# One core: the sixth expert's low parts move from GpSimd to VectorE, and the sorted tokens are routed earlier

## What is computed

```
x = conv_attention(x)               # 1x1 convolutions, batch norm, softmax over 256 pixels, plus x
t = tokens(x)                       # 4 x 256 = 1024 tokens of 128 numbers
t = t + attention(layer_norm(t))    # causal mask, softmax over the queries
t = t + experts(layer_norm(t))
x = images(t)

def experts(z):                     # 8 experts of 128 -> 512 -> 128; each token uses its best 2
    logits = z @ Wg
    top, index = top_k(logits, 2);  w = softmax(top)
    out = 0
    for e in range(8):
        out += cw[:, e] * (silu(z @ W1[e]) @ W2[e])   # cw: w where e was chosen, otherwise 0
    return out
```

## Time and profile before

| what | value |
|---|---|
| median of 3 runs | 128.77 us |
| the three runs | 128.94, 127.63, 128.77 us |
| the profiled execution's own time | 127.66 us |
| its span, first to last instruction | 125.9 us |
| PE busy | 106.8 us, 85% |
| VectorE busy | 91.7 us, 73% |
| ACT busy | 80.5 us, 64% |
| GpSimd busy | 56.0 us, 44% |
| TensorE clock granted | 1.00 in every stage |

### The profile page before, as it was taken

How to read it: one execution, slowest core, us unless ns; L and a number is a source line. 1 busy time by engine, 2 the same in 40 slices (tenths; PEclk the granted TensorE clock), 3 DMA queues, 4 the chain that set the end, 5 groups by cost and what they waited for, 6 DMA issues and landing times.

```text
span 125.9 us, 3269 instructions
## 1 busy us (share of the span) xinstructions
PE 106.8 (85%) x1077; PEld 86.4 (69%) x1077; DVE 91.7 (73%) x310; ACT 80.5 (64%) x193; POOL 56.0 (44%) x96
## 2 busy tenths in 40 slices
PE   5568589699976999999999299689799999999760
PEld 1366469587865599898887177488678877878530
DVE  0264778898799984999476956978998878876720
ACT  4226998548666767988968278657375757575511
POOL 6835752849988500007778845303303330332000
PEclk9999999999999999999999999999999999999999
DMA  2338999970000000000121158000010000000003
GB/s 84 100 88 244 317 343 332 299 175 3 5 0 0 0 0 5 3 0 22 43 68 44 43 131 239 0 0 0 28 43 3 5 0 0 5 0 5 0 0 104
DMA packets 12549, 8.75 MB, mean 70 GB/s; under 512 B 1139, under 2 KB 11350, under 8 KB 12534
## 3 DMA queue, kind: packets, MB, share of 16 engines
q1 hardware_dynamic: 12070, 7.86, 22.1%
q0 software_dynamic: 416, 0.68, 1.7%
q10 hardware_dynamic: 48, 0.02, 0.1%
HBM read 6.20 MB, written 2.35 MB: 68 GB/s over the span
## 4 chain that ended last, share of the span: by engine, by line
PE 43%; DVE 24%; issue 12%; POOL 11%; ACT 5%; DMA 2%; POOLq 0%; ACTq 0%; DVEq 0%
PE bank L1628 7%; POOL rows_dram L677 6%; PE bank L1614 5%; PE bank L1602 3%; PE bank L1604 3%; PE bank L1603 3%; POOL fg L696 2%; DMA xT<-in_x_dram 2%; PE bank L1618 2%; PE bank L1661 2%; DVE acc L1311 2%; DVE st L993 2%; PE bank L1705 2%; PE bank L1707 2%; PE bank L1706 2%
## 5 line engine op out<-in xcount | busy, mean ns | idle before, releaser
L688 POOL TENSOR_TENSOR hidl<-hid,hidh 128x512 f16<-128x512 f32 x8 | 9.2, 1154 | 26.6 <-ACT hid L837 26.6
L835 ACT ACTIVATE hidh<-bank 128x512 f16<-128x512 f32 x17 | 10.2, 597 | 14.0 <-PE bank L1604 13.9
L677 POOL DMA_INDIRECT rows_dram<-rows,slot_at x10 | 11.4, 1135 | 16.1 <-issue 16.1
L1602 PE MATMUL bank<-zg,W1h 128*128 128x128 f16 x68 | 12.6, 220 | 1.6 <-DVE zg L1238 1.6
L1661 PEld LDWEIGHTS bank<-W2f,hid 128*128 128x128 f32 x96 | 12.8, 192 | 1.0
L1661 PE MATMUL bank<-W2f,hid 128*128 128x128 f32 x96 | 13.3, 275 | 0.0
L881 ACT ACTIVATE hid<-bank 128x384 f32<-128x384 f32 x22 | 10.7, 489 | 3.4 <-PE bank L1707 2.3
L1603 PE MATMUL bank<-zg,W1h 128*128 128x128 f16 x68 | 12.6, 219 | 0.0
L1604 PE MATMUL bank<-zg,W1l 128*128 128x128 f16 x68 | 12.6, 219 | 0.0
L878 ACT ACTIVATE hidh<-bank 128x384 f16<-128x384 f32 x16 | 7.8, 489 | 5.4 <-PE bank L1707 4.1
L1614 PE MATMUL bank<-W2hl,hidh 128*128 (+1 forms) x68 | 10.6, 275 | 0.8 <-DVE outl L1263 0.8
(11 more groups left out here) (261 smaller groups left out, 356.0 us busy)
## 6 DMA issues: line engine op xcount, KB each, us to landing
W1f<-in_L_ffn_W_dram SPq DMA_DIRECT2D x8, 256.0 KB, 5.4
W2f<-in_L_ffn_W_dram SPq DMA_DIRECT2D x8, 256.0 KB, 6.0
rows_dram<-zero_row SPq DMA_DIRECT2D x1, 1122.0 KB, 10.1
xg<-rows_dram SPq DMA_DIRECT2D x3, 264.0 KB, 3.7
xT<-in_x_dram SPq DMA_DIRECT2D x2, 256.0 KB, 2.9
out_dram<-total SPq DMA_DIRECT2D x3, 128.0 KB, 1.8
xg<-rows_dram SPq DMA_DIRECT2D x1, 198.0 KB, 2.9
rows_dram<-rows,slot_at POOLq DMA_INDIRECT x10
```

The source lines that it names most:

```text
L677: pool.indirect_dma_start(out=rows_dram[:, :], out_offset=bass.IndirectOffsetOnAxis(ap=slot_at[:, k, i:i + 1], axis=0), in_=rows[:, i, :], ...
L835: act.activation(hidh[:, n % HB, :], pUP[n % 2][:, :], ACT.Silu, scale=1.0 / (XS * WS)).then_inc(high_ready, 1)
L1602: pe.matmul(o, W1h[:, e, ch], zg[:, n % XR, 0:P], start=True, stop=False)
```

## The change

Two things are changed. `POOL_LOW` begins at expert 6 in place of 5, so the low parts of units 20 and 22 (the sixth expert, number 5 from zero, chunks 0 and 2) are made by VectorE from the PSUM bank, and ACT writes their full copies there. And the orders are rewritten: `finalT:3` comes one unit sooner, `route_half` two and `places` two on PE; `turned_copy:3` on ACT stands before unit 4 and `tanh:0` behind it; on VectorE the slots come before other work.

```diff
-    POOL_LOW = tuple((e, c) for e in range(5, E) for c in (0, 2))
+    POOL_LOW = tuple((e, c) for e in range(6, E) for c in (0, 2))
...
     TENSOR_ORDER
-        finalT:2 unit:3 unit:4 finalT:3 unit:5 unit:6 route_half:0 unit:7 unit:8 unit:9 places:0
+        finalT:2 unit:3 finalT:3 unit:4 route_half:0 unit:5 unit:6 unit:7 places:0 unit:8 unit:9
...
     SCALAR_ORDER
-        unit:3 tanh:0 unit:4 turned_copy:3 rows_high:1 unit:5 rows_high:2 rows_high:3 unit:6
+        unit:3 turned_copy:3 unit:4 tanh:0 rows_high:1 unit:5 rows_high:2 rows_high:3 unit:6
...
     VECTOR_ORDER
-        add1:3 stats1:3 aggr1:3 route_copy:0 norm1:2 top_two:0 norm1:3 one_hots:0 weights_low:2
-        gate_tokens:0 rows_low:1 rows_low:2 rows_low:3 top_two_half:0 chosen:0 unit:6 weights_low:3
-        down_weights_low:0 first_slots:0 slots:0 gate_slots:0 blocks:0 unit:10 weights_low:4
+        add1:3 stats1:3 aggr1:3 route_copy:0 norm1:2 norm1:3 top_two:0 one_hots:0 weights_low:2
+        top_two_half:0 chosen:0 gate_tokens:0 unit:6 first_slots:0 slots:0 rows_low:1 rows_low:2
+        rows_low:3 gate_slots:0 weights_low:3 blocks:0 unit:10 down_weights_low:0 weights_low:4 down_weights_low:1 down_weights_low:4 unit:14 weights_low:5 unit:16 unit:17 unit:18
...
     GPSIMD_ORDER
-        rstd1:2 rstd1:3 scatter:0 scatter:1 scatter:2 scatter:3 scatter:4 unit:20 unit:22 unit:24 unit:26
-        unit:28 unit:30"""
+        rstd1:2 rstd1:3 scatter:0 scatter:1 scatter:2 scatter:3 scatter:4 unit:24 unit:26 unit:28 unit:30"""
```

More of the change, by code:

```diff
@@ L135, in conv_attention_moe_kernel @@
         norm1:1 rec1:3 scale_values:3 add1:2 tokens_low:0 stats1:2 tokens_low:1 aggr1:2
-        add1:3 stats1:3 aggr1:3 route_copy:0 norm1:2 top_two:0 norm1:3 one_hots:0 weights_low:2
-        gate_tokens:0 rows_low:1 rows_low:2 rows_low:3 top_two_half:0 chosen:0 unit:6 weights_low:3
-        down_weights_low:0 first_slots:0 slots:0 gate_slots:0 blocks:0 unit:10 weights_low:4
-        down_weights_low:1 down_weights_low:4 unit:14 weights_low:5 unit:16 unit:17 unit:18
+        add1:3 stats1:3 aggr1:3 route_copy:0 norm1:2 norm1:3 top_two:0 one_hots:0 weights_low:2
+        top_two_half:0 chosen:0 gate_tokens:0 unit:6 first_slots:0 slots:0 rows_low:1 rows_low:2
+        rows_low:3 gate_slots:0 weights_low:3 blocks:0 unit:10 down_weights_low:0 weights_low:4 down_weights_low:1 down_weights_low:4 unit:14 weights_low:5 unit:16 unit:17 unit:18
         down_weights_low:5 unit:19 unit:20 weights_low:6 unit:21 unit:22
```

## The result

The changed kernel takes 124.59 us (median of 124.58, 124.58, 125.56 and 124.59), the kernel before, beside it, 128.86 us (128.94, 127.63, 128.77 and 129.22). The ratio is 0.970 (95% interval 0.963 to 0.978), a gain of 3.8 us of 128.86 (2.8 to 4.8); by the two medians it is 4.3. The forecast was 125.6 us: a gain of 2.7 us taken off 128.25. Profile against profile it is 127.66 to 124.58, 3.1 us.

The account below looks back on a forecast made before the run. PE was taken to set the pace, except for a stall set by GpSimd's queue. The lows gain 2.68 us, the orders 0: 128.25, the middle of two run levels, less 2.68 gives 125.6 us, range 124.6 to 127.4.

Parts of the forecast that it names:

- The stall: PE idle before unit 24, waiting for GpSimd's low of unit 20 queued behind the scatters; removing it gains 2.68 us.
- VectorE covers the two lows: In expert 5, VectorE's four lows, one addition and two weight lows take 3.92 us where PE takes 3.96.
- Rival 1: VectorE becomes the bound around unit 24, its weight low held up; time 126.5 to 126.9 us; chance 8%.
- Who holds whom: VectorE instructions with two SBUF inputs and GpSimd's SBUF reads exclude each other; a scatter might hold `weights_low:6`, costing 0.2 us.
- the row of 2.79 us: `weights_low:7` on VectorE in the earlier profile, ending at 73.50 beside GpSimd's lows; taken as a sign of mutual exclusion.
- Part 2: The rewritten orders: scatters end 1.45 us sooner, but worth 0, and cost 0 if unit 12 isn't kept.
- rival 2: Row halves and slots keep expert 3's weights late at unit 12, losing 0.5 to 1 us: about 126.3; chance 5%.
- rival 3: The gain is hidden: `turn:0` and slot gates wait for loads that stay in place; 126.9 us; chance 5%.
- Slower, by late scatters: Stretched scatters delay GpSimd's low of unit 24 and PE waits; 130.1 us with an end at 77; chance 4%.
- threshold of 72.5: Latest time in us at which GpSimd may start the low of unit 24 without making PE wait.
- The step that failed is the sum: Whole-kernel time: 127.66 - 2.68 = 124.98 us against the profiled execution, 125.6 us from the middle level of runs.
- the lower end of the range, 124.6: Whole-kernel time at the low level of runs, with 0.4 us in case a wait behind the stall shrinks too.

Follow-up runs that it names:

- the repetition: The changed kernel once more, unchanged, on a second chip beside the kernel before: 125.12 us, ratio 0.970.
- The turned blocks first: Changed kernel with VectorE's last steps reordered, the first turned block's copy ahead of unit 31's low and two weight lows earlier: 124.10 us, ratio 0.961.

## Why the prediction was right, and what it missed

- *The stall* (2.68): right. Unit 24 at 69.53, 2.68 sooner measured from unit 12; no wait took its place.
- *VectorE covers the two lows*: right, within 0.13 us at each step (67.16 for 67.25; unit 23's low at 70.99 for 71.10; the low of unit 25 done at 73.09 for 73.2). The 3.92 of 3.96 held, and with all four further lows on VectorE it still did. Rival 1 is refuted.
- *Who holds whom*: the row of 2.79 us had two possible holders. Now `weights_low:6` started at 67.64 beside a scatter (67.25 to 68.21) and took 0.68, so this scatter didn't hold it; four more profiles have the same overlap and the same 0.68. `weights_low:7` took 1.17 and ended at 72.62, 0.54 behind GpSimd's low, as forecast: a low of GpSimd holds it. The 2.79 ended 0.56 behind the second of GpSimd's lows, too. But that row began at 70.71, 0.45 before the first of them (71.16), and at its usual 0.68 it would have had 0.23 left; what kept it over these 0.45 us, beside the last scatter, no run shows. By the Trainium skill ("SBUF — State Buffer", Who interferes with whom) I had a cut of 0.2 us by a scatter as holder; no run here shows that cut. That GpSimd's lows hold it agrees with the page.
- *Part 2 worth nothing*: right, and shown by taking it away (124.59 with the lows alone). Router at 46.05 (46.2), places 50.55 (50.65), first scatter 55.39 (55.6), last end 69.47 (69.7), expert 3's weights ready at 54.95 (55.1), unit 12 not kept: rival 2 is refuted, and so is rival 3: the loads were issued from 70.8 to 72.8 and took up to 5.2 us, so they were there by 78.0, before VectorE read them at 79.65, and the `zg` wait stayed at 1.6. The ten scatters are as long as forecast (14.08), by chance: one took 2.55 and the others less.
- *Slower, by late scatters*: the mechanism is real and its threshold of 72.5 was right, but it takes 3 us more of delay to reach it than there was (scatters ending at 72.5, for 69.47). Even 0.7 beyond it the kernel was 2.3% faster (1.9 to 2.8).
- *The term that was missed.* The step that failed is the sum, where I left the two levels of runs, 127.65 and 128.85, without a cause and gave both to the new kernel. The upper level is mostly part of the stall: in most runs of the kernel before TensorE falls to 1.2 GHz behind it and loses 1.3 to 1.6 us more. The stall's price is 2.7 in a run without the fall and 4.0 to 4.3 with it, and the changed kernel loses both. In numbers the forecast was 1.0 too high: 0.6 for the middle level (128.25 less the profiled 127.66), and 0.4 that is the scatter of single profiles (the 0.10 and 0.3 above). The median lies on the lower end of the range, 124.6, which I had given another reason. The mechanism was right, the size of this term wrong.
- *Luck.* That the changed kernel's median stood at its lower level, 124.58, is in part luck: it has dearer runs of its own, from another fall, one of four here and two of four in the repetition, whose median is 125.12.

Not settled: why either fall comes in some runs and stays out in others, whether the unprofiled dearer runs of the changed kernel have theirs at 40 us, and what held PE, ACT and VectorE near 70 us on the first chip.

## What to carry to other kernels

A profile taken at full clock hides what a stall costs in the usual run: compare the profiled execution's time and mean clock with the other runs before making a sum. Where they stand above it, take a second profile of such a run and see where its clock is low; only what lies behind the stall belongs to its price. When one of two edits already turns a wait into slack, the other adds nothing to it; try each alone, since the cheaper one may do (here one table entry), and the next gain is at the next wait (`zg`, 0.5 to 1.2 us of span by order alone).

## What the runs showed of the hardware

- Behind a PE wait of 2.5 us the granted clock went to 0.50 for about 3.4 us, though PE was busy throughout, and then back to 1.00 (one profile; 27 of 30 runs of that kernel have a mean clock of 0.973 to 0.987). It did so once behind a wait of 2.1, in one of five runs, and behind one of 0.9 in none of four. It also fell at 40 us, for about as long, in two profiles in which PE had been busy for 2.55 and 2.44 of the 4 us before and had waited at most 0.70 us at a time; in the twelve other profiles, with PE busy for 2.42 to 2.66 us of that stretch, the clock stayed at 1.00.
- A scatter's issue took 2.55 us where most take 0.96, with VectorE making three weight lows (two inputs in SBUF) without a pause. Their rows in the changed kernel:

```profile
56.05 0.67 DVE L1297 SCALAR_TENSOR_TENSOR W2hl<-W2f,W2hl 128x512 f16<-128x512 f32 x1
56.65 0.67 DVE L1291 SCALAR_TENSOR_TENSOR W1l<-W1f,W1h 128x512 f16<-128x512 f32 x1
57.25 1.27 DVE L1297 SCALAR_TENSOR_TENSOR W2hl<-W2f,W2hl 128x512 f16<-128x512 f32 x2
```

  The scatter ran from 56.83 to 59.38 and ended 0.86 us behind the last of them (58.52). The second scatter took 2.54 or 2.55 us in all seven profiles with this order and no delay in front of it, and 1.34 or 1.35 in the four with VectorE's order of before; the longest of any scatter there is 1.47. The stretched scatters of the kernel before follow the same pattern: those of 1.34, 1.26, 1.36 and 1.47 us each began while a weight low was under way, and ended 0.83 to 0.85 us behind it (the last: 71.14, behind 70.30). Together they add 1.6 us, as much as the one of 2.55 alone, so the ten took the same 14.1 us. A weight low and a low of GpSimd hold each other up as well. In two places the one that began second was held: the weight low of 1.17 for 0.68 above, and in *The turned blocks first* GpSimd's low begun at 77.21, 0.13 behind a weight low of 0.68, which took 1.32 for 0.91. The row of 2.79, which began 0.45 first and was held, doesn't fit that order. A scatter holding a weight low was not seen at 67.64. What it is that the two engines share no run here shows.
- ACT stood still for 3.5 to 6.8 us and PE and VectorE did little (in the worst stretch 1.38 and 0 of 4 us), while GpSimd's scatters went on, with no engine and no line named as the cause: in all four profiles on one chip, and in none of eight on the two others.
